# Sums of even and odd key blocks added on the way out of PSUM, and the output projection in row tiles of 64, in 25 of 32 heads

## What is computed

```python
h = _layernorm(x, ln1_g, ln1_b)
q, k, v = (h @ wq), (h @ wk), (h @ wv)            # per head: 1024 x 64
attn = softmax(einsum('bihd,bjhd->bhij', q, k) * scale)
out = einsum('bhij,bjhd->bihd', attn, v).reshape(B, S, D_ATTN)
x = out @ wo + bo + x                             # then cross attention, feed-forward
```

## Time and profile before

| | |
|---|---|
| median of 3 runs | 1064.27 us (1063.29 to 1068.29) |
| the profiled execution | 1063.16 us, of which the span from first to last instruction is 1061.4 |
| PE busy (matmuls) | 1025.7 us, 97% of the span |
| DVE, ACT, POOL busy | 828.3 (78%), 626.0 (59%), 300.7 (28%) |
| self attention | from about 30 to 785 us of the span |

### The profile page before, as it was taken

How to read it: one execution, slowest core, us unless ns; L and a number is a source line. 1 busy time by engine, 2 the same in 40 slices (tenths; PEclk the granted TensorE clock), 3 DMA queues, 4 the chain that set the end, 5 groups by cost and what they waited for, 6 DMA issues and landing times.

```text
span 1061.4 us, 28582 instructions
## 1 busy us (share of the span) xinstructions
PE 1025.7 (97%) x12258; PEld 834.4 (79%) x12258; DVE 828.3 (78%) x971; ACT 626.0 (59%) x1127; POOL 300.7 (28%) x268
## 2 busy tenths in 40 slices
PE   7989999999998999999999999998999999999998
PEld 5777777777776778777777777876688888888887
DVE  4768888889889878888888889999768898555433
ACT  4746665666676656666666666676655645443322
POOL 5103322322332123423223222322313336711000
PEclk9999999999999999999999999999999999999999
DMA  8897677667666956575785657598210001100001
GB/s 188 235 199 166 136 152 156 125 134 139 144 134 122 204 121 141 116 161 119 147 183 115 140 119 153 116 213 182 47 62 21 1 11 40 51 1 20 20 2 40
DMA packets 179646, 121.38 MB, mean 114 GB/s; under 512 B 142656, under 2 KB 159552, under 8 KB 175040
## 3 DMA queue, kind: packets, MB, share of 16 engines
q1 hardware_dynamic: 179520, 119.55, 51.6%
HBM read 56.60 MB, written 12.58 MB: 65 GB/s over the span
## 4 chain that ended last, share of the span: by engine, by line
PE 81%; DVE 8%; ACT 5%; issue 3%; POOL 1%; DMA 1%; SPq 0%; DVEq 0%; POOLq 0%; ACTq 0%
PE W L622 21%; PE SC L597 18%; PE W L634 10%; PE SC L686 8%; PE W L570 7%; PE W L696 4%; PE W L580 4%; PE W L862 3%; ACT OTF L950 3%; PE SC L674 2%; DVE nmax L1164 2%; DVE PR L1169 2%; PE W L849 1%; ACT PR L942 1%; POOL PR L512 1%
## 5 line engine op out<-in xcount | busy, mean ns | idle before, releaser
L942 ACT ACTIVATE PR<-SC,nmax 128x1024 f32<-128x1024 f32 x256 | 285.8, 1116 | 224.4 <-DVE nmax L1164 223.9
L1164 DVE TENSOR_REDUCE nmax<-SC 128x1 f32<-128x1024 f32 x256 | 308.2, 1204 | 108.3 <-PE SC L597 108.1
L1169 DVE STREAM_TRANSPOSE PR<-PR 128x1024 f32<-128x1024 f32 x256 | 315.2, 1231 | 0.1
L464 POOL TENSOR_TENSOR X<-f_raw,X 128x512 f32<-128x512 f32 x128 | 164.9, 1289 | 498.3 <-ACT f_raw L961 498.2
L597 PE MATMUL SC<-QKS 128*128 128x512 f32 x1024 | 297.1, 416 | 4.9 <-ACT PR L942 4.8
L622 PE MATMUL W<-PR,V 32*64 32x256 f32 x8192 | 240.2, 379 | 4.4 <-DMA V<-scratch_v 2.4
L597 PEld LDWEIGHTS SC<-QKS 128*128 128x128 f32 x1024 | 184.2, 188 | 64.9 <-issue 23.0
L622 PEld LDWEIGHTS W<-PR,V 32*64 32x64 f32 x8192 | 187.0, 132 | 51.3 <-issue 23.9
L634 PE MATMUL W<-wo,OTF 128*128 128x256 f32 x512 | 134.4, 385 | 7.9 <-ACT OTF L950 7.0
L634 PEld LDWEIGHTS W<-wo,OTF 128*128 128x128 f32 x512 | 93.9, 189 | 36.9 <-ACT OTF L950 20.7
L961 ACT ACTIVATE f_raw<-W,rden 128x256 f32<-128x256 f32 x256 | 106.5, 473 | 0.1
(11 more groups left out here) (128 smaller groups left out, 1401.5 us busy)
## 6 DMA issues: line engine op xcount, KB each, us to landing
QKS<-QKT SPq DMA_DIRECT2D x64, 512.0 KB, 6.3
V<-scratch_v SPq DMA_DIRECT2D x128, 256.0 KB, 5.0
QKS<-QKT SPq DMA_DIRECT2D x128, 128.0 KB, 4.8
scratch_v<-VST SPq DMA_DIRECT2D x32, 256.0 KB, 4.7
wo<-in_L_xattn_sa_wo_dram SPq DMA_DIRECT2D x64, 64.0 KB, 3.0
f_raw<-in_L_xattn_ff_w_dram SPq DMA_DIRECT2D x12, 256.0 KB, 3.1
X<-in_x_dram SPq DMA_DIRECT2D x4, 512.0 KB, 5.0
w_raw<-in_L_xattn_sa_wk_dram SPq DMA_DIRECT2D x16, 128.0 KB, 2.9
```

The source lines that it names most:

```text
L464: nc.gpsimd.tensor_tensor(xs, f_raw[:, k % 2, :], xs, ALU.add).then_inc(p_x, 1)
L942: nc.scalar.activation(PR[:, NT * s + t, :], SC[t % 2][:, :], ACT.Exp, bias=nmax[:, t % 4:t % 4 + 1], accum_out=den[:, s, t:t + 1]).then_i ...
L1164: V.tensor_reduce(nmax[:, t % 4:t % 4 + 1], SC[t % 2][:, :], AX, ALU.max, negate=True).then_inc(d_max, 1)
L1169: V.transpose(tile, tile).then_inc(d_tr, 1)
```

## The change

In every head except 0, 11, 12, 13, 14, 29 and 30 (PLAIN):

- P\*V of odd key blocks goes to columns 128 to 383 of its bank instead of 0 to 255. So columns 128 to 255 hold the even blocks' second half of the queries on partitions 0 to 63, and the odd blocks' first half on partitions 64 to 127.
- The gather is two ScalarE copies of 64 x 512 that bring the other two quarters to the opposite partitions, into the second half of OTF, and then one VectorE addition (`add_halves`) of PSUM columns 128 to 255 and these copies into the first half of OTF: 128 x 512, with four query tiles on each half of the partitions.
- The output projection (`project_sums`) is eight matmuls of 64 rows, in turns on the array's upper and lower 64 rows and into different banks, all in one place after scores 6.
- Scale-out 0 and 1 both come ahead of exponential 6, scale-out 2 and 3 both in step 0 of the next period. Waits of the projections for free banks follow that.

In all periods from head 1 on, VectorE does turn 2 ahead of row maximum 3, and in periods with the new form turn 4 ahead of row maximum 5, with the addition behind it. Behind the last head all four parts are projected in the new form, and the V\*W products that reuse the banks wait for each scale-out. At the start SyncE issues the store of the cross attention's values (L342) after the loads of V for heads 0 and 1 instead of before. Comments and empty lines are left out:

```diff
@@ -114,7 +115,7 @@
         WB = [TP[1], TP[0], MISC, PV]
-        MB = [MISC, PV, TP[0], TP[1]]
+        MB = [PV, TP[1], TP[0], MISC]
@@ -170,8 +171,22 @@
+        PLAIN = (0, 11, 12, 13, 14, 29, 30)
         STEPS = {5: 0, 6: 1, 7: 2}
-        OUT_BANK = (2, 1, 0, 1)
+        def out_tile(h, k):
+            return 2 * k if h in PLAIN else (4, 0, 6, 2)[k]
+        def out_bank(h, k):
+            return ((2, 1, 0, 1) if h in PLAIN else (2, 1, 0, 3) if h == HS - 1 else (3, 2, 1, 0))[k]
+        def summed(h):
+            return sum(g not in PLAIN for g in range(h + 1))
@@ -338,11 +353,11 @@
                 store_v(0, i)
-            sp.wait_ge(a_pre, 8)
-            sp.dma_start(KV_d[1], flat(14, 2)).then_inc(m_kvs, 16)
             stored(0)
...
             load_v(1)
+            sp.wait_ge(a_pre, 8)
+            sp.dma_start(KV_d[1], flat(14, 2)).then_inc(m_kvs, 16)
@@ -460,7 +475,7 @@
                         pool.wait_ge(p_xb, 2 * (h // NH) + 2)
-                    xs = X[:, h // NH, 2 * k:2 * k + 2, :].rearrange("p t d -> p (t d)")
+                    xs = X[:, h // NH, out_tile(h, k):out_tile(h, k) + 2, :].rearrange("p t d -> p (t d)")
                     nc.gpsimd.tensor_tensor(xs, f_raw[:, k % 2, :], xs, ALU.add).then_inc(p_x, 1)
@@ -617,23 +633,38 @@
                     cols = slice(DH * (blk % 2), DH * (blk % 2) + DH)
+                    on = 0 if h in PLAIN else P * (blk % 2)
                     for a in range(4):
                         rows = slice(Q * a, Q * a + Q)
-                        last = mm(W[cols, a, 0:2 * P], V4[s][rows, blk, :],
+                        last = mm(W[cols, a, on:on + 2 * P], V4[s][rows, blk, :],
                                   PR[rows, NT * s:NT * s + NT, Q * blk:Q * blk + Q],
...
                 if k == 0:
-                    pe.wait_ge(a_ot, h + 1)
+                    pe.wait_ge(a_ot, h + 1 + summed(h))
                     pe.wait_ge(m_wo[h % 2], 32 * (h // 2 + 1))
...
                     t = 2 * k + i
-                    last = mm(W[:, OUT_BANK[k], D * i:D * i + D], OTF[:, t * P:(t + 1) * P], wo2[h % 2][:, :],
+                    last = mm(W[:, out_bank(h, k), D * i:D * i + D], OTF[:, t * P:(t + 1) * P], wo2[h % 2][:, :],
                               start=True, stop=True)
                 last.then_inc(s_op, 1)
+            def project_sums(h):
+                pe.wait_ge(d_ot, summed(h))
+                pe.wait_ge(m_wo[h % 2], 32 * (h // 2 + 1))
+                for n in range(4):
+                    for c in range(2):
+                        rows = slice(DH * c, DH * c + DH)
+                        last = mm(W[:, out_bank(h, 2 * (n // 2) + c), D * (n % 2):D * (n % 2) + D],
+                                  OTF[rows, n * P:(n + 1) * P], wo2[h % 2][rows, :], start=True, stop=True)
+                        if n % 2:
+                            last.then_inc(s_op, 1)
@@ -722,8 +753,10 @@
                         attend(h - 1, BURSTS[t])
-                    if h > 0 and t in STEPS:
+                    if h - 1 in PLAIN and t in STEPS:
                         project_out(h - 1, STEPS[t])
+                    if h > 0 and h - 1 not in PLAIN and t == 6:
+                        project_sums(h - 1)
                     if (h, t) == (0, 4):
@@ -734,7 +767,7 @@
                         elif t == 1:
-                            pe.wait_ge(a_op, 4 * (h - 2) + 3)
+                            pe.wait_ge(a_op, 4 * (h - 2) + (3 if h - 2 in PLAIN else 4))
                         project_v(u, i, W[:, bank, :])
@@ -742,7 +775,9 @@
                         elif t == 0:
-                            pe.wait_ge(a_op, 4 * (h - 2) + 1)
+                            pe.wait_ge(a_op, 4 * (h - 2) + (1 if h - 2 in PLAIN else 2))
+                        elif h > 0 and h - 1 not in PLAIN:
+                            pe.wait_ge(a_op, 4 * (h - 1) + 1)
                         elif h == 0 and t < 7:
@@ -768,12 +803,14 @@
                             pe.wait_ge(m_caq, 16)
-                        if i % 2:
-                            pe.wait_ge(a_op, 4 * (h - 2) + 1)
+                        if i < 2:
+                            pe.wait_ge(a_op, 4 * (HS - 4) + i + 1)
+                        elif i == 3:
+                            pe.wait_ge(a_op, 4 * (HS - 3) + 1)
                         if i >= 2:
...
                         turn_wq(i, bank)
-                    if t == 0 and h > 1:
+                    if t == 0 and h - 2 in PLAIN:
                         pe.wait_ge(a_op, 4 * (h - 2) + 2)
@@ -791,15 +828,11 @@
             ca_scores(1)
-            for k in range(4):
-                if k == 3:
-                    pe.wait_ge(a_op, 4 * (HS - 1) + 2)
-                project_out(HS - 1, k)
+            project_sums(HS - 1)
             pe.wait_ge(m_vb[0], 16)
...
             for j in range(4):
-                if j > 0:
-                    pe.wait_ge(a_op, 4 * (HS - 1) + (0, 1, 3, 4)[j])
+                pe.wait_ge(a_op, 4 * (HS - 1) + j + 1)
                 make_vw(0, j, MB[j])
@@ -944,23 +977,30 @@
                     act.wait_ge(s_op, 4 * h)
-                nc.scalar.copy(OTF[:, :].rearrange("p (t a i) -> p a t i", a=4, i=Q),
-                               W[:, :, 0:2 * P].rearrange("p a (t i) -> p a t i", i=Q)).then_inc(a_ot, 1)
+                if h in PLAIN:
+                    nc.scalar.copy(OTF[:, :].rearrange("p (t a i) -> p a t i", a=4, i=Q),
+                                   W[:, :, 0:2 * P].rearrange("p a (t i) -> p a t i", i=Q)).then_inc(a_ot, 1)
+                else:
+                    for to, of, col in ((DH, 0, 0), (0, DH, 2 * P)):
+                        nc.scalar.copy(OTF[to:to + DH, BANK:2 * BANK].rearrange("p (a n) -> p a n", a=4),
+                                       W[of:of + DH, :, col:col + P]).then_inc(a_ot, 1)
...
                 n = 4 * h + k
-                act.wait_ge(s_op, n + 1)
+                act.wait_ge(s_op, n + 1 if h in PLAIN else 4 * h + 2 * (k // 2) + 2)
                 if k == 0:
...
                 for i in range(2):
-                    done = nc.scalar.mul(f_raw[:, k % 2, D * i:D * i + D],
-                                         W[:, OUT_BANK[k], D * i:D * i + D],
-                                         rden[:, h % 2, 2 * k + i:2 * k + i + 1])
+                    t = out_tile(h, k) + i
+                    done = nc.scalar.mul(f_raw[:, k % 2, D * i:D * i + D], W[:, out_bank(h, k), D * i:D * i + D],
+                                         rden[:, h % 2, t:t + 1])
                 done.then_inc(a_op, 1)
@@ -1022,10 +1062,16 @@
                         gather(h - 1)
-                    if t in (6, 7) and h > 0:
+                    if t in (6, 7) and h - 1 in PLAIN:
                         scale_out(h - 1, t - 6)
-                    if t in (0, 1) and h > 1:
+                    elif t == 6 and h > 0:
+                        scale_out(h - 1, 0)
+                        scale_out(h - 1, 1)
+                    if t in (0, 1) and h - 2 in PLAIN:
                         scale_out(h - 2, 2 + t)
+                    elif t == 0 and h > 1:
+                        scale_out(h - 2, 2)
+                        scale_out(h - 2, 3)
                     for g, n, bank in proj_before(h, t):
@@ -1168,6 +1214,14 @@
+            def add_halves(h):
+                dve.wait_ge(a_ot, h + 1 + summed(h))
+                dve.wait_ge(s_op, 4 * h)
+                V.tensor_tensor(OTF[:, 0:BANK].rearrange("p (t a i) -> p a t i", a=4, i=Q),
+                                W[:, :, P:2 * P].rearrange("p a (t i) -> p a t i", i=Q),
+                                OTF[:, BANK:2 * BANK].rearrange("p (a t i) -> p a t i", a=4, i=Q), ALU.add).then_inc(d_ot, 1)
             def invert(h):
@@ -1249,11 +1303,18 @@
                 for t in range(NT):
+                    summing = h > 0 and h - 1 not in PLAIN
+                    if h > 0 and t == 3:
+                        turn(h, 2)
                     rowmax(h, t)
...
                         split_qkv(g, n, W[:, bank, :])
-                    if t > 0 or h > 0:
+                    if (t > 0 or h > 0) and not (t == 3 and h > 0 or t == 5 and summing):
                         turn(*divmod(NT * h + t - 1, NT))
+                    if t == LAST_BURST and summing:
+                        turn(h, t)
+                        add_halves(h - 1)
                     if h > 0 and t == 1:
@@ -1301,6 +1362,7 @@
                 split_m(0, j, SCB[j])
+            add_halves(HS - 1)
             ca_sub(0)
...
             ca_sum(0)
```

More of the change, by code:

```diff
@@ L155, in build_block @@
         s_sc = sem("s_sc"); d_max = sem("d_max"); a_exp = sem("a_exp"); d_tr = sem("d_tr"); d_rd = sem("d_rd")
-        s_pv = sem("s_pv"); a_ot = sem("a_ot"); s_op = sem("s_op"); a_op = sem("a_op")
+        s_pv = sem("s_pv"); a_ot = sem("a_ot"); d_ot = sem("d_ot"); s_op = sem("s_op"); a_op = sem("a_op")
         s_wt = sem("s_wt"); a_wt = sem("a_wt"); s_m = sem("s_m"); a_m = sem("a_m"); d_m = sem("d_m")
```

## The result

The changed kernel takes 1050.76 us (median of 4 runs, 1050.46 to 1052.94) against 1064.61 for the kernel before: **ratio 0.9876, 95% interval 0.9857 to 0.9895**, 13.8 us less. The forecast was 1038, that is 26 us less: the sign was right, the size about double.

The account below looks back on a forecast made before the run. Heads were taken as bound by TensorE. Gains of 20.9 (heads), 4.0 (start), 1.0 (plain periods) and 0.6 (end) sum to 26.5 us: 1063.16 becomes 1036.7, or 1038 for the median of runs; range 1025 to 1056.

Parts of the forecast that it names:

- The row tiles: Output projection on TensorE: sixteen records in two row tiles run together, 1.74 us per head instead of 3.48.
- What is late next: Ordinary periods: after the change ScalarE's chain from gather to exp 0 is late, the period 22.05 us instead of 23.20.
- the term of 20.9 us for the heads: Summed gain over 20 periods with new form and V projection; seventeen full ones, at 1.15 us each, give 19.6.
- copies 9.45 to 10.55: Gather on ScalarE: two copies start when burst 2 ends, 9.45 us after the first burst, and take until 10.55.
- the copy of OTF starts at 9.67, as exp 4 ended only at 9.60: Gather in the kernel before: exponential 4 holds up the copy, though the second burst's sums are readable at 9.39 us.
- the 1.0 of the plain periods: Five plain periods gain 0.2 us each from the earlier gather that turn 2 ahead of row maximum 3 allows.
- They gain 0: New-form periods without a V projection already sit at 22.01 us, on the same chain, so they gain nothing.
- The bn_stats periods: Two periods with eight bn_stats: VectorE's load would be 22.8 of 23.34 us with the addition, so 0.3 gained each.
- The start: First burst, with V loads ahead of the KV store: 2.36 us wait and 1.69 of slow clock go, 4.0 gained.
- The tail: Behind the last head: projection shrinks by 1.24 us, V*W blocks 2 and 3 wait for multiplies, 0.6 kept.
- Rival 4: Only the start counts as said, a transfer or VectorE is late in some periods: 1048 us; chance 0.15.
- Rival 1: Handover's copies, addition and multiplies take 1.15 us more, period stays 23.2: 1058.7 us, or 1061.7; chance 0.12.

Follow-up runs that it names:

- e5: Kernel after with row maximum 5 ahead of VectorE's addition: 1059.95 us, ratio 0.9968 against the kernel before.
- e6: Kernel after with multiply pair 1 (scale-out 1) behind exponential 6 instead of ahead of it: 1053.42 us, ratio 0.9886 against the kernel before.
- e7: e6 with multiply pair 3 (scale-out 3) also moved behind exponential 0, pairs 2 and 3 exchanging banks: 1045.37 us, ratio 0.9810 against the kernel before.
- e2: e1 plus turn 2 ahead of row maximum 3 in every head after the first, plain form everywhere: 1061.53 us, ratio 0.9988 against the kernel before.
- e10: The kernel after, unchanged, run again on one chip with e11: 1053.25 us, ratio 0.9893 against the kernel before.
- e1: Kernel before with only SyncE's store of the cross attention's values moved behind the loads of V: 1061.67 us against 1063.88, ratio 0.9984.
- e4: Kernel after with heads 8 and 25 to 28 in the plain form too: 1049.49 us, ratio 0.9870 against the kernel before.
- e9: Kernel after with every matmul of the sums' projection issued twice, same result: 1084.52 us, ratio 1.0190 against the kernel before.
- e3: Kernel after with the eight 64-row matmuls in runs of two on the same array half instead of in turns: 1054.15 us, ratio 0.9928 against the kernel before.
- e11: The e7 kernel run again, on one chip with e10: 1047.04 us, ratio 0.9837 against the kernel before.
- e8: e7 with heads 26, 27 and 28 in the plain form as well: 1045.24 us, ratio 0.9826 against the kernel before.

## Where the forecast was right, and which step failed

- **The row tiles.** Taken as both together, 1.74 us; measured 2.00 with the tail of the last record, starts 216 ns apart in pairs. Right. The Trainium skill (TensorE: Matmul & The Clock Gate, Part 3, Measured speedup vs the span model) has measured a speedup of 3.07 for four row tiles, which would have made it an estimated 2.27. The trace does not agree for two tiles of 64: in steady flow they lost nothing.
- **What is late next.** ScalarE's chain from gather to exponential 0: right. e5 (+0.35 where 0.35 was expected), e6 (0) and e7 (-0.38 where -0.5 was) each moved the period as that chain says. The page on tiling (Trainium skill, TensorEngine Tiling (Array Packing), PSUM Bottleneck) says that copying out of PSUM may become the bottleneck once tiling has made TensorE faster. This trace agrees in kind: the copies (1.19 us) and the addition (0.69) out of PSUM stand in the chain that is late now, and scores wait 50.7 us for exponentials after 10.1.
- **The step that failed**, in the term of 20.9 us for the heads: "copies 9.45 to 10.55", and with it "the copy of OTF starts at 9.67, as exp 4 ended only at 9.60". The two times lie 0.07 apart, and I took the nearer one for the cause. e2 moved exponential 4 away and the copy stayed: it waits for the burst's own signal, 4.0 us after the burst began (3.71 had been taken). The copies took 1.19, not 1.08. Together 0.23 + 0.1 in a chain with no slack, 0.36 per period: the 1.15 was 0.79. Over 17 periods that is 6.1 of the 16.3 us missing; the same step takes away the 1.0 of the plain periods. Another 1.9 went in two of the 17 (heads 23 and 24), to pauses of TensorE with nothing to wait for: their second bursts took 4.36 and 4.51 us instead of 3.71. Scores 3 of head 24 also began 0.75 late; why isn't clear. e10, the same program, lost only 0.5 in the two periods.

```profile
570.92 4.36 PE L639 MATMUL W<-PR,V 32*64 32x256 f32 x128
...
594.53 3.68 PE L639 MATMUL W<-PR,V 32*64 32x256 f32 x120
598.38 0.66 PE L639 MATMUL W<-PR,V 32*64 32x256 f32 x8 [0.17 <-issue]
```

- **"They gain 0", for periods without V.** They sat on the old chain at 22.01 and came under the new one, which is 0.4 to 0.5 longer. In head 28's, VectorE has two small operations of the next layer norm (L1236, L1238) ahead of row maximum 7, and with no slack left exponential 7 comes 0.74 later; the gather, 9.68 after the burst, is where it always is:

```profile
690.11 1.19 ACT L990 COPY OTF<-W 64x512 f32<-64x512 f32 x2 [0.17 <-PE W L639]
...
695.79 0.72 DVE L1238 SCALAR_TENSOR_TENSOR mr<-mv,rs 128x8 f32<-128x8 f32 x1
...
697.68 1.12 ACT L975 ACTIVATE PR<-SC,nmax 128x1024 f32<-128x1024 f32 x1 [0.73 <-DVE nmax L1210]
```

At head 29, TensorE's wait of 1.99 us was followed by half clock, in e10 the same wait was not. +4.0 instead of 0 (+2.1 in e10). I had reckoned waits of TensorE at their own length and not at what the clock does behind them, though the earlier trace rows showed exactly that at the start.
- **The bn_stats periods** grew by 0.2 instead of shrinking by 0.3: I compared sums of VectorE's load, but the added work stands in the chain. In the period of head 9 exponential 4 ends only just before the gather, which starts 10.22 after the burst instead of 9.68, and exponential 7 comes at 17.67 instead of 16.51. In e7, with ScalarE's part shorter, the period falls to 22.71.
- **The start.** Wait and slow burst went as forecast. 2.2 us in e1 and 2.3 after, not 4.0, and the likely reason is a fall of the clock earlier in those executions: in e1 and the kernel after the core ran at half clock for a part of the stretch between 10 and 16 us of the span (0.50 from 12 to 14), in the profiled execution before it did not. e2 and e4, without that fall, reached head 2 at 82.85 and 82.67, 3.3 to 3.5 ahead of before. So the term was about right for an execution with no such fall. That isn't the whole of it: e9 had the fall too and reached head 2 at 82.31, and the second burst of head 1, with pauses inside, took between 4.16 us (e6) and 7.51 (e5).
- **The tail:** 0.2 of 0.6, probably since ScalarE's multiplies stand between projection and V\*W; no run took it apart.
- Rivals: none took place of the forecast as a whole. Rival 4, "about half the gain, 1048", is nearest in time and partly in mechanism. Rival 1 named the place that failed, the chain of the handover; it asked for 1.15 us more there, and 0.36 came.

## What to carry to other kernels

When an engine's work shrinks, the gain ends at the next chain, and a chain without slack passes on every tenth of a microsecond of each handover, times the number of periods: so take the start of its first link from what releases it (the same handover elsewhere in the trace), not from a duration, and not from the event that happens to end nearest. Price a new wait of TensorE with the half clock that may follow it. And where two pieces of one engine's work stand ahead of what the critical engine needs, put only what is needed ahead: here moving two pairs of multiplies behind exponentials gave 6 us more with the same work.

## What the runs showed of the hardware

- Row tiles of 64 run fully side by side whether their matmuls alternate (2.00 us for sixteen records) or come in runs of two per tile (2.10): with four records in a row on one half of the array, the other half still starts beside it (in e3 too the first two records start 13 ns apart).
- A burst's completion reaches another engine 4.00 us after the first of its 128 records, though the last record is shown as ended at 3.71. In the traces of the kernel after and of e2 to e11, 21 or more gathers each, for which ScalarE stood idle, start at 4.00 (within 0.02).
- In several profiled executions TensorE stopped in the middle of a burst with nothing to wait for. The timeline of e10:

```profile
481.05 0.66 PE L639 MATMUL W<-PR,V 32*64 32x256 f32 x8 [3.02 <-issue]
```

It came at head 19 in e6, e7, e8, e10 and e11, and cost 5 us with the half clock behind it, but not in the first profile of the same program as e10; e11 has a second one, of 3.15 us, at head 29. In all six one packet of 16 KB of the profile's instruction queue (q8) starts 0.3 to 0.7 us after TensorE stopped and takes 0.9 to 1.2, and TensorE goes on 1.3 to 1.5 after its end. In e10, the DMA queues from 477.9 to 481.1:

```profile
q8 instruction: 1, 0.02, 1.9%
```

So code that reached TensorE late is a candidate. It isn't shown: such packets also fall into bursts that don't stop, and no run took it apart.
